# Second attention: the top-64 search of wide score tiles in pairwise maxima and minima

## What is computed

```python
    k = jnp.concatenate([mem_k, k], axis=2)            # 16 memory keys before the 512 keys
    dots = jnp.einsum('bhid,bhjd->bhij', q, k) * scale
    dots = jnp.einsum('bhij,hk->bkij', dots, pre_proj) # mixes the 16 heads
    dots = jnp.where(causal, neg, dots)
    top = lax.top_k(dots, 64)[0]
    vk = top[..., -1:]                                 # the 64th largest of each row
    dots = jnp.where(dots < vk, neg, dots)
    attn = jax.nn.softmax(dots, axis=-1)
```

## Time and profile before

| | |
|---|---|
| time, median of 3 runs | 3853.56 us |
| the profiled execution, its own time | 3853.54 us |
| its span in the profile | 3851.7 us |
| DVE busy in the span | 2491.4 us (65%), 7770 instructions |
| PE busy in the span | 2838.4 us (74%) |
| POOL busy in the span | 976.2 us (25%) |
| second attention, the stretch of its searches | about 1190 to 2675 us |
| MATCH_REPLACE8 (L2062), all | 1540 instructions, 605.2 + 104.0 us |

### The profile page before, as it was taken

How to read it: one execution, slowest core, us unless ns; L and a number is a source line. 1 busy time by engine, 2 the same in 40 slices (tenths; PEclk the granted TensorE clock), 3 DMA queues, 4 the chain that set the end, 5 groups by cost and what they waited for, 6 DMA issues and landing times. The chain is left out here.

```text
span 3851.7 us, 40732 instructions
## 1 busy us (share of the span) xinstructions
PE 2838.4 (74%) x11696; PEld 1831.2 (48%) x11696; DVE 2491.4 (65%) x7770; ACT 1078.0 (28%) x2754; POOL 976.2 (25%) x1217
## 2 busy tenths in 40 slices
PE   4755993699658667766776777555325989999999
PEld 1323562477544345544554555444112437666666
DVE  4995565355132999899989999997694334311112
ACT  1102551244113333333333343322100012321221
POOL 2550001100202444545454544453002220000000
PEclk7656996899866788778777868676656999999999
DMA  2000003455412111121212121110001031212112
GB/s 87 0 0 15 6 1 114 135 165 165 153 53 94 67 60 64 60 82 47 75 47 88 43 80 60 56 31 5 16 0 64 0 85 30 85 53 82 60 53 69
DMA packets 181179, 235.88 MB, mean 61 GB/s; under 512 B 35929, under 2 KB 139037, under 8 KB 180702
## 3 DMA queue, kind: packets, MB, share of 16 engines
q1 hardware_dynamic: 177886, 224.88, 18.1%
q0 software_dynamic: 3072, 8.39, 0.7%
HBM read 171.08 MB, written 62.13 MB: 61 GB/s over the span
## 5 line engine op out<-in xcount | busy, mean ns | idle before, releaser
L2062 DVE MATCH_REPLACE8 a_rest<-a_best,a_rest 128x416 f32<-128x416 f32 (+54 forms) x1308 | 605.2, 471 | 0.0
L2070 DVE MAX8 a_best<-a_rest 128x8 f32<-128x416 f32 (+54 forms) x1308 | 566.5, 475 | 0.0
L1745 PE MATMUL a_pat<-a_kp,a_probs 128*128 128x128 f32 x1344 | 295.7, 395 | 206.1 <-POOL a_kp L1964 201.1
L1745 PEld LDWEIGHTS a_pat<-a_kp,a_probs 128*128 128x128 f32 x1344 | 262.4, 291 | 287.5 <-POOL a_kp L1964 263.4
L2003 POOL TENSOR_SCALAR a_probs<-a_mixed,a_best 128x120 f32<-128x120 f32 (+12 forms) x208 | 286.2, 1376 | 331.0 <-DVE a_best L2074 302.2
L1726 PE MATMUL a_psc<-a_kT,branch 64*128 64x264 f32 (+3 forms) x640 | 228.7, 616 | 153.8 <-ACT a_stage L1828 153.2
L3037 DVE TENSOR_TENSOR tl_hT<-tl_act_out,tl_gate 128x512 f32<-128x512 f32 x128 | 88.6, 692 | 385.9 <-ACT tl_act_out L2905 385.8
L1736 PE MATMUL a_pmix<-a_rows,a_kpre 128*128 128x264 f32 (+41 forms) x528 | 185.4, 480 | 84.9 <-ACT a_mixed L1861 80.2
L2819 PE MATMUL tl_py<-tl_w,tl_hT 128*128 128x256 f32 x1024 | 241.6, 379 | 0.0
L2800 PE MATMUL tl_ph<-xT,tl_w 128*128 128x512 f32 x512 | 240.6, 592 | 0.0
L1726 PEld LDWEIGHTS a_psc<-a_kT,branch 64*128 64x128 f32 x640 | 119.4, 262 | 246.1 <-ACT a_stage L1828 220.3
(11 more groups left out here) (421 smaller groups left out, 5307.5 us busy)
## 6 DMA issues: line engine op xcount, KB each, us to landing
f_w<-in_L_ffn_W SPq DMA_DIRECT2D x39, 1024.0 KB, 5.6
tl_gate<-l_gates SPq DMA_DIRECT2D x256, 128.0 KB, 2.9
l_scores<-a_stage SPq DMA_DIRECT2D x32, 528.0 KB, 2.7
l_scores<-a_stage SPq DMA_DIRECT2D x32, 400.0 KB, 2.4
l_scores<-a_stage SPq DMA_DIRECT2D x32, 272.0 KB, 2.1
f0o_w<-in_L_ffn_W SPq DMA_DIRECT2D x8, 1024.0 KB, 12.6
sorted_x<-z_blank SPq DMA_DIRECT2D x1, 4992.0 KB, 17.0
f_xs<-sorted_x SPq DMA_DIRECT2D x39, 128.0 KB, 5.2
```

The lines of the kernel that those rows point to most:

```text
L1745: ins = pe.matmul(pat[:, at + c, :], probs[:, g % 4, c * P:(c + 1) * P], kp[:, g % 4, :], start=True, stop=True)
L2062: last[a] = signal(dve.match_replace(rest[:, a, 0:wd], best[:, a, q - 1, :], rows_of[a] if q == 1 else rest[:, a, 0:wd], GONE))
L2070: last[a] = signal(dve.max(best[:, a, q, :], rest[:, a, 0:wd]))
```

## The change

Pairs whose even tile has 344 columns or more (`halved`) are searched by a new routine, `search_halves`. With h = half the width, it writes the larger of x[j] and x[j+h] into the first half of `rest` and the smaller into the second: two TENSOR_TENSORs on `mixed`. The 64 largest of the row are then among the 64 largest of the first half and the 32 largest of the second, since each minimum has a maximum that is no smaller. So it takes 8 rounds of MAX8 (7 MATCH_REPLACE8) in the half of maxima and 4 rounds (3 MATCH_REPLACE8) in that of minima, each over h columns. The two sorted lists are joined: a TENSOR_TENSOR takes 33 minima of the last 33 maxima, reversed, and the list of minima with a +3e38 ahead of it, and a TENSOR_REDUCE takes the largest of the 33, which is the 64th value. It raises `found`. `top_ready` is raised for both lanes at once, after the first MAX8 of both halves of both lanes. At its start the routine waits until both `found` of the pair before are there.

```diff
+        HALVED = 344
+        def halved(g):
+            return l1_tile(g)[3] >= HALVED
...
+                def search_halves(pair, lanes):
+                    last = {}
+                    if searches(2 * pair):
+                        dve.wait_ge(found, searches(2 * pair))
+                    for a, g, wd in lanes:
+                        dve.wait_ge(cut_done, g + 1)
+                        if g >= 2:
+                            dve.wait_ge(neg_ready, g - 1)
+                        h = wd // 2
+                        x, y = mixed[:, g % DEEP, 0:h], mixed[:, g % DEEP, h:wd]
+                        last[a, 0] = signal(dve.tensor_tensor(rest[:, a, 0:h], x, y, ALU.max))
+                        last[a, 1] = signal(dve.tensor_tensor(rest[:, a, h:wd], x, y, ALU.min))
+                    for q in range(LAST + 1):
+                        for a, g, wd in lanes:
+                            h = wd // 2
+                            for part in range(2 if 2 * q <= LAST else 1):
+                                values = rest[:, a, part * h:part * h + h]
+                                if q:
+                                    top = best[:, a, q - 1, :] if part == 0 else low[:, a, 8 * q - 7:8 * q + 1]
+                                    after(last[a, part])
+                                    last[a, part] = signal(dve.match_replace(values, top, values, GONE))
+                        for a, g, wd in lanes:
+                            h = wd // 2
+                            for part in range(2 if 2 * q <= LAST else 1):
+                                values = rest[:, a, part * h:part * h + h]
+                                after(last[a, part])
+                                if q == LAST and searches(g - 1):
+                                    dve.wait_ge(masked, searches(g - 1))
+                                ins = dve.max(best[:, a, q, :] if part == 0 else low[:, a, 8 * q + 1:8 * q + 9], values)
+                                last[a, part] = signal(ins)
+                        if q == 0:
+                            after(last[lanes[-1][0], 1])
+                            dve.sem_inc(top_ready, 2)
+                        if q == TOP1 // 16 and pair >= 2:
+                            invert(pair - 2)
+                    for a, g, wd in lanes:
+                        top = best[:, a].rearrange("p q e -> p (q e)")
+                        after(last[a, 0])
+                        last[a, 0] = signal(dve.tensor_tensor(both[:, a], top[:, TOP1 // 2 - 1:TOP1][:, ::-1], low[:, a],
+                                                              ALU.min))
+                    for a, g, wd in lanes:
+                        after(last[a, 0])
+                        dve.tensor_reduce(best[:, a, LAST, 7:8], both[:, a], AX.X, ALU.max).then_inc(found, 1)
...
                 for pair in range(PAIRS1):
...
+                    if halved(2 * pair):
+                        search_halves(pair, lanes)
+                        continue
```

More of the change, by code:

```diff
@@ L1529, in l1_attention @@
         least = sb("least", [P, 2])
+        low = sb("low", [P, 2, 1 + TOP1 // 2])
+        both = sb("both", [P, 2, 1 + TOP1 // 2])
         probs = sb("probs", [P, 4, CH1 * P])
@@ L2033, in invert @@
                     dve.reciprocal(rden[:, x], den[:, x]).then_inc(inverted, 1)
+                after(signal(dve.memset(low[:, :, 0:1], -GONE)))
                 for pair in range(PAIRS1):
```

## The result

The changed kernel takes 3847.5 us (median of 9 runs, 3838.89 to 3852.0), the kernel before 3854.72 on the same occasions: a ratio of 0.9978 with a 95% interval of 0.9968 to 0.9988. So the change brings 0 to 0.3%, where 4012 us and a slower kernel had been forecast. The profiled execution has a span of 3849.1 us.

The account below looks back on a forecast made before the run. DVE was taken to bound the second attention's searches. From the profiled 3853.5 us, 22 us of gain and a 181 us stall against POOL made + 159, so 4012 us; range 3826 to 4040.

Parts of the forecast that it names:

- two cases: Range 3826 to 4040 us: taking turns with DVE first (4012 us, chance 0.47) and no stall (3832 us, 0.28).
- What bounds the kernel: Second attention's searches: DVE is always busy, so its gain or loss in 48 changed pairs reaches the span one to one.
- excluded PE: Rival that PE or ACT becomes the bound: ruled out, as no pair gets shorter by more than 1 us.
- The price of DVE's instructions: DVE in the searches: 1.042 ns a column, about 0.06 us fixed per instruction, 0.068 us per value load.
- the 22: Net gain without contention over the 48 changed pairs: 130.8 us gained by columns, 109 lost to fixed costs and waits.
- The stated bounds, 12 to 32: Gain in us over the 48 pairs without contention, between the bounds of the added waits.
- What the new TENSOR_TENSORs meet: At a changed pair's start, DVE's four TENSOR_TENSORs and POOL's compares and adds wait out each other's whole instructions: 181 us stall.
- DVE first and then turns: DVE's first TENSOR_TENSOR passes; second to fourth wait for both compares and lane 0's add: 4012 us, chance 0.47.
- No contention: Rival at the pair starts: no stall, or DVE keeps its turn through its four instructions; 3832 us, chance 0.28.
- POOL first: Rival: POOL precedes DVE everywhere, then turns, so DVE waits for the fourth POOL instruction too: 46 us more, 4058, chance 0.12.

Follow-up runs that it names:

- all three edits: Changed kernel with POOL's compare held until DVE's four TENSOR_TENSORs end, top_ready raised by the MAX8 itself, no found wait behind halved pairs: 3782.68 us, 0.9926 of the kernel before.
- meets the adds: Changed kernel whose four TENSOR_TENSORs also wait for both POOL compares, so that they meet POOL's adds: 4079.39 us (1 run), kernel before 3850.57.
- compare as TENSOR_TENSOR: Changed kernel with POOL's compare, a TENSOR_SCALAR, replaced by a TENSOR_TENSOR (x - x), mask left out: 3939.93 us (1 run), kernel before 3852.24.
- top_ready by MAX8: Changed kernel in which the first MAX8 of each lane's maxima raises top_ready itself: 3800.47 us, 0.9968 of the kernel before.
- no wait for found: Changed kernel in which a pair behind a halved pair skips the wait for both found before its first TENSOR_TENSOR: 3805.25 us, 0.9980 of the kernel before.

## Why the prediction was wrong

The measured time lies inside the stated range, but only because the range spans two cases; the likelier of them, a kernel slower by 159 us, was the wrong one, and the direction with it.

**What bounds the kernel** held for the change: DVE is without idle time to speak of at the changed pairs, and what they gained, less the 2.6 us beside them, moved the stretch. It no longer held one to one once more was gained: with all three edits the pairs take 35.9 us less and the stretch 29, since PE is the bound where the batch changes. The prediction had excluded PE by the windows of blocks 3 and 2, which do not reach over that place.

**The price of DVE's instructions** held. All in all, 3.5 us of the 22 were missed: `top_ready` costs 0.25 a pair for 0.15 (4.8 us too little; the share of the semaphore step in it had stood on no row), against which the join costs 0.57 ahead of a changed pair and 0.45 ahead of another, for 0.58. The stated bounds, 12 to 32, hold 18.5; but by the prediction's own 0.9 us a pair for the join the lower one is 6.5 and not 12.

**The step that failed is the length of POOL's hold in "What the new TENSOR_TENSORs meet".** The two rows that showed DVE waiting out a whole instruction of POOL were both of a TENSOR_TENSOR on POOL, and the compare is a TENSOR_SCALAR. The prediction named that gap and carried the rule over it. In the same place a TENSOR_TENSOR makes DVE wait 2.2 us a pair (104 / 48), the compare 0.25 (12.0 / 48); the sum had 181 / 48 = 3.8. DVE's second passes, the third waits 0.40 us for a compare of 1.98. Since the compare lets go early, DVE's four are over before the second compare starts (at pair 47 they end at 1737.22, and it starts at 1735.39 + 4.58 - 2.00 = 1737.97), and the waits for the compare of lane 1 and for the add of lane 0 never happen. The form of the sum, DVE first and then turns, holds: the kernel with TENSOR_TENSORs in the compare's place shows it row by row.

By the Trainium skill ("SBUF — State Buffer", section "Who interferes with whom", and the row on both engines in its summary) the second to issue is blocked for the whole instruction. For POOL's TENSOR_TENSOR the traces agree (1.40 us for 0.40); for its TENSOR_SCALAR they don't (0.13 to 0.40 us lost to records of 1.4 to 2.5 us), and the measurement decides.

**The rivals.** "No contention" gave 3832 and had the right sign; it lacked the 12 us of the third TENSOR_TENSOR, the 3.5 us above and the 2.6 us at the pairs beside the changed ones. With these its 22 us become some 4, against 7.2 and 2.4 in the medians. "POOL first" did happen, at the first pair of block 2 and, by 0.05 us, at that of block 3, and cost 0.13 and 0.09 us.

**What stays open.** Why a TENSOR_SCALAR of POOL holds the operand only at first is not shown; that it reads its own operand in at 0.83 ns a column and then works for the rest fits the slope, and no more. Whether it is the operation or the number of its SBUF operands that decides is open as well; a TENSOR_SCALAR and a TENSOR_TENSOR are all that was tried. At block 2's first pair the first TENSOR_TENSOR loses only 0.13 us, where 0.83 ns for each of 328 columns would be 0.27; the compare had begun 0.25 us ahead of it there, so that a part of the hold may have been over, which was not tested.

## What to carry to other kernels

A stall seen between two engines is a price for that pair of operations: before it is taken over to another operation, ask whether the row shows the same one, and if not, keep the small end of its price among the likely cases. Splitting wide searches into halves saves columns and pays in instructions and in waits, so waits that an engine makes on its own last instruction (0.13 to 0.25 us each here) weigh in where the threshold lies; in the pairs they were worth 17.4 us, the change itself 5.1. Where a collision can be had out of the way by ordering work of the engine that has slack, as POOL's compare here, try that first: at the pairs it gave back the whole stall. And when the bound of a stretch gets faster, look at its seams too, where another engine may be just behind.

## What the runs showed of the hardware

- POOL's TENSOR_SCALAR of one SBUF operand makes a two-operand DVE instruction wait 0.27 us at 344 columns of POOL's and 0.40 at 504 (the change), though its own record is 1.45 and 1.98 us long. POOL's TENSOR_TENSOR makes it wait to its end: 1.40 us for 0.40 at 236 columns, ending 0.26 us after POOL's ("meets the adds").
- The hold works both ways: the compare of 504 columns takes 2.50 us for 1.98 when it starts beside DVE's TENSOR_TENSORs.
- With both engines pending and a TENSOR_TENSOR on each, they take turns even when DVE's instructions follow each other without a wait: 0.82, 0.83 and 1.05 us lost at the second, third and fourth ("compare as TENSOR_TENSOR").
- Waiting for its own last MAX8 and stepping a semaphore costs DVE 0.23 us (0.57 for 0.34, "top_ready by MAX8"); waiting for its own last TENSOR_REDUCE 0.13 (5.3 us in 40 pairs, "no wait for found").
